# The long filters' matrices re-laid in pairs of steps, and loaded by the rows that have taps

## The reference

```python
v = silu(dwconv(x @ Wv, conv_v))          # q and k likewise
paths = [dwconv(v, fir_s), dwconv(v, fir_m), dwconv(v, fir_l), delta_path, v]
# dwconv: y[t, c] = sum over i of w[c, i] * x[t - (K - 1) + i, c], per channel; K = 3, 15, 64
```

## Time and profile before

| | us |
|---|---|
| median of 3 runs | 971.71 (969.2 to 977.56) |
| the profiled execution | 980.14 |
| its span | 978.3 |
| TensorE busy | 870.4 (89% of the span) |
| TensorE's granted clock over the span | 0.952 of full |
| L666, start of the first to end of the last | 119.0 to 171.7 |

### The profile page before, as it was taken

How to read it: one execution, slowest core, us unless ns; L and a number is a source line. 1 busy time by engine, 2 the same in 40 slices (tenths; PEclk the granted TensorE clock), 3 DMA queues, 4 the chain that set the end, 5 groups by cost and what they waited for, 6 DMA issues and landing times.

```text
span 978.3 us, 18379 instructions
## 1 busy us (share of the span) xinstructions
PE 870.4 (89%) x6875; PEld 654.3 (67%) x6875; DVE 605.2 (62%) x1410; ACT 453.0 (46%) x845; POOL 345.7 (35%) x336
## 2 busy tenths in 40 slices
PE   7799789789999987998889888979997999999994
PEld 5577566667777765786556555656785777777774
DVE  5799797566889888432557777774462343333255
ACT  5788656446677766342144544445331322222221
POOL 9422200123557566312001343223540242222684
PEclk9999999778999997998799999999999999999998
DMA  5699769897455432124991222002302222221421
GB/s 168 202 269 281 203 153 250 296 240 172 109 119 120 76 76 78 32 86 165 388 338 42 63 63 88 12 24 80 100 23 83 66 60 60 66 66 50 151 65 64
DMA packets 144468, 123.52 MB, mean 126 GB/s; under 512 B 89790, under 2 KB 126590, under 8 KB 143102
## 3 DMA queue, kind: packets, MB, share of 16 engines
q1 hardware_dynamic: 140974, 112.98, 41.0%
q0 software_dynamic: 3408, 9.38, 2.6%
HBM read 74.04 MB, written 48.29 MB: 125 GB/s over the span
## 4 chain that ended last, share of the span: by engine, by line
PE 60%; DVE 14%; ACT 10%; POOL 7%; issue 4%; DMA 3%; SPq 1%; POOLq 0%; DVEq 0%; ACTq 0%; another core or an unknown queue 0%
PE ps L2513 10%; PE ps L1919 6%; PE ps L2528 5%; DVE cross_room L1952 4%; PE ps L1859 3%; PE ps L2377 3%; PE ps L1352 3%; PE ps L666 3%; PE ps L1620 3%; POOL hank L345 2%; PE ps L1981 2%; POOL kept L2660 2%; PE ps L2390 2%; PE ps L423 2%; DMA hank<-rt_dram 2%
## 5 line engine op out<-in xcount | busy, mean ns | idle before, releaser
L1997 ACT ACTIVATE cross_room<-ps 128x1024 f32<-128x1024 f32 x64 | 65.5, 1023 | 99.1 <-PE ps L1923 96.9
L1952 DVE TENSOR_REDUCE cross_room<-ps 128x4 f32<-128x1024 f32 x64 | 78.1, 1224 | 39.3 <-PE ps L1919 38.5
L2513 PE MATMUL ps<-wr,xbT 128*128 x312 | 99.0, 459 | 1.8 <-ACT xbT L2549 1.8
L1919 PE MATMUL ps<-kept,cross_room 32*128 32x256 f32 x512 | 74.1, 411 | 21.7 <-DVE cross_room L1952 18.8
L2602 POOL DMA_INDIRECT y_dram<-yb,dest_row x39 | 37.5, 961 | 134.6 <-DVE dest_row L2578 130.4
L1320 POOL TENSOR_TENSOR st<-st,exponent 128x20 f32<-128x20 f32 x16 | 56.9, 3554 | 64.7 <-DVE st L1295 63.4
L2513 PEld LDWEIGHTS ps<-wr,xbT 128*128 128x128 f32 x312 | 58.8, 189 | 29.5 <-issue 2.5
L1923 PE MATMUL ps<-cross_room,kept 32*128 32x256 f32 x512 | 75.3, 413 | 0.0
L1919 PEld LDWEIGHTS ps<-kept,cross_room 32*128 32x128 f32 x512 | 47.1, 190 | 39.7 <-issue 21.7
L550 DVE SCALAR_TENSOR_TENSOR room<-room 128x256 f32<-128x256 f32 x144 | 58.4, 480 | 11.4 <-ACT room L499 11.4
L2587 DVE TENSOR_TENSOR cross_room<-cross_room,ps 128x352 f32<-128x352 f32 x39 | 20.3, 521 | 58.6 <-PE ps L2513 57.1
(11 more groups left out here) (353 smaller groups left out, 2243.2 us busy)
## 6 DMA issues: line engine op xcount, KB each, us to landing
xs_dram<-params SPq DMA_DIRECT2D x17, 1040.0 KB, 17.9
room<-in_gW SPq DMA_DIRECT2D x8, 1280.0 KB, 7.7
tok_dram<-room SPq DMA_DIRECT2D x8, 768.0 KB, 6.4
fir_dram<-room SPq DMA_DIRECT2D x6, 1024.0 KB, 7.3
paths<-fir_dram SPq DMA_DIRECT2D x48, 128.0 KB, 3.7
xb<-xs_dram SPq DMA_DIRECT2D x39, 130.0 KB, 2.3
hank<-rt_dram SPq DMA_DIRECT2D x8, 512.0 KB, 8.1
yr<-y_dram SPq DMA_DIRECT2D x16, 256.0 KB, 3.2
```

The lines of the kernel that those rows point to most:

```text
L1919: m1 = nc.tensor.matmul(ps[:, c, t * T:(t + 1) * T], strips(qS[b % 3], g, c)[:, t * P:(t + 1) * P], kS(b, g)[c * CH:(c + 1) * CH], start=T ...
L1952: V.tensor_reduce(mx[:, :, g, XD + 2 * h * CH:XD + (2 * h + 1) * CH + 1:CH].rearrange("p t c -> p c t"), ps[:, pair(h), :].rearrange("p c ...
L1997: S.activation(pT[g % 2][:, pair(h)].rearrange("p c k t -> p (c k t)"), ps[:, pair(h), :].rearrange("p c n -> p (c n)"), ACT.Exp).then_inc ...
L2513: m = nc.tensor.matmul(ps[:, 2 * (j % 2) + half, 0:FF], xbT[j % 2][:, k, :], wr[:, bass.ds(e, 1), k, half, :].rearrange("p e n -> p (e n)" ...
```

## The change

The 64 steps of a block become 4 blocks of `PER` = 16 steps (index a), each of 8 pairs (index i) of two steps 8 apart (index h): step = 16 a + i + 8 h. `hank` is [128, a, filter, i, channel, h], so that the two steps of a pair are adjacent floats; `rt_dram` rows are twice as wide, holding tap n and tap n + 8 of each channel. The transposes and copies of the filters double to twelve (the second six from `wpad` shifted by 8). The filters lie in `tok[1]` for that time, which gives two new waits in batch 1, and `pe_project` waits for the copies in batch 1 as a third bank is used. A slice is loaded by eight DMAs, four blocks x (64-tap filter; the two short ones), each over the rows in which a filter has taps in that block. The copy out of PSUM and the stores of `stage` follow the new order.

```diff
+LAG = 8
+PER = 2 * LAG
+STEPS_A = BLK // PER
-HANK = ((2, 1, 0, 32), (2, 1, 32, 96), (2, 1, 96, P), (0, 2, 48, 64), (0, 2, 64, 96), (0, 2, 96, P))
+HANK = tuple((f, count, step, P - FIRS[f + count - 1] - PER * step - PER + 1, P - PER * step)
+             for step in range(STEPS_A) for f, count in ((2, 1), (0, 2)))
...
-        filters = views(room3, 0, n_filters, "p (k r f c) -> p k r f c", k=KT, r=RING, f=NF)
-        wpad = views(room3, n_filters, n_filters, "p (k f n) -> p k f n", k=KT, f=NF)
+        filters = tok[1].rearrange("p t j d -> p (t j d)").rearrange("p (k r f c) -> p k r f c", k=KT, r=RING, f=NF)
+        wpad = views(room3, 0, n_wpad, "p (k f n) -> p k f n", k=KT, f=NF)
...
+            pe.wait_ge(s.raw_copied, 3)
+            for n in range(FILTERS):
+                h, k, f = n // (KT * NF), n // NF % KT, n % NF
+                m = nc.tensor.transpose(filter_bank(n), wpad[:, k, f, h * LAG:h * LAG + P], ident[:])
...
+                if j == 2 and b == 1:
+                    pe.wait_ge(s.filters_copied, FILTERS)
...
+            if b == 1:
+                act.wait_ge(s.filters_out, FILTERS_OUT)
             S.copy(tok[i][:, :, 2, :], ps[:, 6, :].rearrange("p (t d) -> p t d", t=TT)).then_inc(*s.v_copied.up())
...
+            if b == 1:
+                dve.wait_ge(s.filters_out, FILTERS_OUT)
...
-                nc.sync.dma_start(env.fir_dram[f, c * NCH:(c + 1) * NCH].rearrange("q (n t) d -> (q n) (t d)", t=BLK),
-                                stage[c][:, f].rearrange("p t d -> p (t d)")).then_inc(*env.fir_out.up(16))
+                nc.sync.dma_start(env.fir_dram[f, c * NCH:(c + 1) * NCH].rearrange("q (n a t) d -> (q n) a (t d)", a=STEPS_A, t=PER),
+                                stage[c][:, :, NF - 1 - f].rearrange("p a t d -> p a (t d)")).then_inc(*env.fir_out.up(16))
...
-                                                 env.hank[sl % RING][:, :, :, q * SL // NCH + pair * 2 + u].rearrange("k f s -> k (f s)"),
+                                                 env.hank[sl % RING][:, :, :, :, q * SL // NCH + pair * 2 + u].rearrange("k a f i h -> k (a f i) h"),
...
-                    S.copy(stage[sl // RING].rearrange("p f t c -> p c f t")[:, c0:c0 + 2, :, ::-1],
-                           ps[:, sl % 2 * PAIRS + pair, 0:2 * NF * BLK].rearrange("p (c f t) -> p c f t", c=2, f=NF)
+                    S.copy(stage[sl // RING].rearrange("p a f (h i) c -> p c (a f) i h", h=2)[:, c0:c0 + 2, ::-1, ::-1, ::-1],
+                           ps[:, sl % 2 * PAIRS + pair, 0:2 * NF * BLK].rearrange("p (c n i h) -> p c n i h", c=2, i=LAG, h=2)
...
-    for f, count, k0, k1 in HANK:
-        s0, s1 = max(0, P - FIRS[f + count - 1] - k1 + 1), min(BLK, P - k0)
-        src = bass.AP(tensor=rt.tensor, offset=((sl * NF + f) * (P + BLK) + s0 + k0) * SL,
-                      ap=[[SL, k1 - k0], [(P + BLK) * SL, count], [1, (s1 - s0) * SL]])
-        nc.sync.dma_start(env.hank[sl % RING][k0:k1, f:f + count, s0:s1, :].rearrange("k f s c -> k f (s c)"),
+    for f, count, step, k0, k1 in HANK:
+        row = 2 * SL
+        src = bass.AP(tensor=rt.tensor, offset=((sl * NF + f) * (P + BLK) + PER * step + k0) * row,
+                      ap=[[row, k1 - k0], [(P + BLK) * row, count], [1, LAG * row]])
+        nc.sync.dma_start(env.hank[sl % RING][k0:k1, step, f:f + count].rearrange("k f i c h -> k f (i c h)"),
                           src).then_inc(*env.hank_in[sl % RING].up(16))
...
-            env.hank = [mem.enter_context(nc.sbuf_tensor(f"hank{i}", [P, NF, BLK, SL], F32)) for i in range(RING)]
+            env.hank = [mem.enter_context(nc.sbuf_tensor(f"hank{i}", [P, STEPS_A, NF, LAG, SL, 2], F32)) for i in range(RING)]
```

More of the change, by code:

```diff
@@ L259, in phase_project_invert_and_fir @@
         n_conv, n_kt, n_sq, n_diag = 3 * KT * T, KT * TT * P, 2 * TT * D, NP * CH
-        n_stage, n_inv, n_filters = NF * BLK * CH, NG * CH * CH, KT * NF * P
+        n_stage, n_inv, n_wpad = NF * BLK * CH, NG * CH * CH, KT * NF * (P + LAG)
         room0 = sb("room0", [P, n_stage])
@@ L269, in phase_project_invert_and_fir @@
         xT = views(room1, n_raw + 2 * n_tok + 2 * n_x, n_x, "p (k t) -> p k t", k=KT)
-        stage = [views(r, 0, n_stage, "p (f t c) -> p f t c", f=NF, t=BLK) for r in (room0, room1)]
+        stage = [views(r, 0, n_stage, "p (a f t c) -> p a f t c", a=STEPS_A, f=NF, t=PER) for r in (room0, room1)]
         room2 = sb("room2", [P, 2 * n_inv])
@@ L283, in phase_project_invert_and_fir @@
         room3 = sb("room3", [P, n_inv])
-        filters = views(room3, 0, n_filters, "p (k r f c) -> p k r f c", k=KT, r=RING, f=NF)
-        wpad = views(room3, n_filters, n_filters, "p (k f n) -> p k f n", k=KT, f=NF)
+        filters = tok[1].rearrange("p t j d -> p (t j d)").rearrange("p (k r f c) -> p k r f c", k=KT, r=RING, f=NF)
+        wpad = views(room3, 0, n_wpad, "p (k f n) -> p k f n", k=KT, f=NF)
         am = views(room3, 0, n_inv, "p (g i j) -> p g i j", g=NG, i=CH)
-        no_taps = env.hank[0][0:BLK, 0, 0:SLICES * NF, :]
+        no_taps = views(env.hank[0][0:BLK].rearrange("k a f i c h -> k (a f i c h)"), 0, SLICES * NF * 2 * SL, "k (n c) -> k n c", n=SLICES * NF)
+        FILTERS, FILTERS_OUT = 2 * KT * NF, 16 * (KT * RING + 1)
         gw1_rows = a["gW1"][D:, :].rearrange("(n g p) c -> p g n c", n=NPATH, p=P)
@@ L313, in sp_weights, with filter_bank @@
                                   a[f"fir{f}"].rearrange("(k p) i -> p k i", p=P)).then_inc(*s.wpad.up(16))
+        def filter_bank(n):
+            return ps[:, (6, 7, 3)[n // 4], n % 4 * P:(n % 4 + 1) * P]
         def pe_filters():
             pe.wait_ge(s.wpad, 16 * NF)
[L319 to L322, removed]
+            pe.wait_ge(s.raw_copied, 3)
+            for n in range(FILTERS):
+                h, k, f = n // (KT * NF), n // NF % KT, n % NF
+                m = nc.tensor.transpose(filter_bank(n), wpad[:, k, f, h * LAG:h * LAG + P], ident[:])
             m.then_inc(*s.filters_turned.up())
@@ L326, in act_filters @@
             act.wait_ge(s.filters_turned, 1)
[L327 to L330, removed]
+            for n in range(FILTERS):
+                h, k, f = n // (KT * NF), n // NF % KT, n % NF
+                S.copy(filters[:, k, :, f, h::2].rearrange("n r (q c) -> n q r c", q=NCH),
+                       filter_bank(n).rearrange("n (q r c) -> n q r c", q=NCH, r=RING)).then_inc(*s.filters_copied.up())
         def sp_filters():
-            sp.wait_ge(s.filters_copied, KT * NF)
+            sp.wait_ge(s.filters_copied, FILTERS)
             for k in range(KT):
@@ L344, in pool_hank_zero @@
                     pool.in_turn()
-                    G.memset(h[:, f].rearrange("k s c -> k (s c)"), 0.0).then_inc(*pool.tick(env.hank_zero))
+                    G.memset(h[:].rearrange("k a f i c h -> k (a f i c h)")[:, f * BLK * SL:(f + 1) * BLK * SL], 0.0).then_inc(*pool.tick(env.hank_zero))
         def sp_first_hank(sl):
@@ L452, in pe_normalise @@
                     pe.wait_ge(s.win_made, b)
-                    pe.wait_ge(s.filters_copied, KT * NF)
+                    pe.wait_ge(s.filters_copied, FILTERS)
                 for t in range(TT):
@@ L771, in sp_hank @@
     nc, rt = pg.nc, env.rt_dram
-    for f, count, k0, k1 in HANK:
-        s0, s1 = max(0, P - FIRS[f + count - 1] - k1 + 1), min(BLK, P - k0)
-        src = bass.AP(tensor=rt.tensor, offset=((sl * NF + f) * (P + BLK) + s0 + k0) * SL,
-                      ap=[[SL, k1 - k0], [(P + BLK) * SL, count], [1, (s1 - s0) * SL]])
-        nc.sync.dma_start(env.hank[sl % RING][k0:k1, f:f + count, s0:s1, :].rearrange("k f s c -> k f (s c)"),
+    for f, count, step, k0, k1 in HANK:
[3 more added lines that the diff above has]
+        nc.sync.dma_start(env.hank[sl % RING][k0:k1, step, f:f + count].rearrange("k f i c h -> k f (i c h)"),
                           src).then_inc(*env.hank_in[sl % RING].up(16))
-        if k1 == P:
+        if f == 0 and step % 2:
             yield
@@ L2700, in decoder_program @@
         env.beta = env.sb("beta", [P, B, NP])
-        env.rt_dram = nc.dram_tensor("rt_dram", [SLICES, NF, P + BLK, SL], F32).ap()
+        env.rt_dram = nc.dram_tensor("rt_dram", [SLICES, NF, P + BLK, 2 * SL], F32).ap()
         env.fir_out, env.hank_zero, env.hank_in = pg.counter(), pg.counter(), [pg.counter() for _ in range(RING)]
```

## The result

| | us |
|---|---|
| after, median of 4 runs | 1144.6 (1140.9 to 1148.39) |
| before on the same chip, median of 4 runs | 973.41 (969.2 to 977.56) |
| ratio | 1.1753 [1.1703, 1.1804] |
| the profiled execution of after, and its span | 1141.66, 1139.9 |

The account below looks back on a forecast made before the run. The prediction took matmuls, filter loads and VectorE's inversion to bound the stretch before the delta phase. Single-engine loads would delay x, tokens and slices, starting that phase 146 us later: 1,126 profiled, 1,118 median, so 1,120 us, range 1,070 to 1,200.

Parts of the forecast that it names:

- Loads on one engine, the same each time: Filter loads: 79 rows is prime, so each such DMA runs on one DMA engine, always the same.
- The share of 1/16: Sign of being right: DMA engines' share near 1/16 for long stretches between 200 and 310 us.
- several 79-row loads were in flight at once: Sign of being wrong: several of the 79-row filter DMAs in flight at the same time.
- The first rival: Filter loads spread or change engines, nothing slow: delta phase could start at 168.3, median 965, 0.7% faster; chance 0.10.
- 81 ns a packet, 27.0 us a slice: Filter loads: one engine at 25.4 GB/s, 81 ns a packet, needs 27.0 us a slice with the short filters.
- the third rival: Filter loads: the lone engine runs at 13.5 GB/s, 51 us a slice, 1,310 us in all; chance 0.04.
- x of batches 5, 6, 7 at 88.5, 121.5, 155: Projection: x waits on the engine behind slices, so its landings come 15, 35 and 55 us late.
- Slice 4 issued at 202: Filter loads: batch 5's token store is 67 us late, moving slice 4's issue from 134.7 to 202.
- Four slices 108 us, filters' end 315, delta phase 316: Last four filter slices take 108 us; filters end at 315, delta phase starts at 316, 146 us later.
- Later phases unchanged: After the delta phase's start: the later phases keep their times.
- Pairs 41 ns a record: Filters' matmuls on TensorE: paired reads cost 41 ns a record instead of 87, busy time 45.1 to about 21 us.
- VectorE is the floor for any gain: Before the delta phase: VectorE inverts until 167.6, so the phase can't start earlier, whatever the filters gain.

Follow-up runs that it names:

- Experiment 1: The changed kernel with its filter loads over 80 and 32 rows instead of 79 and 30; 976.62 us, ratio 1.0047.
- eighth run: The changed kernel with 80- and 32-row loads and two of VectorE's twelve second-inversion rounds moved into the delta phase; 973.79 us, ratio 0.999.
- experiment 7: The changed kernel with 80- and 32-row loads, two inversion rounds moved into the delta phase and only `hank[0]` cleared up front; 972.41 us, ratio 0.996.

## Why the prediction was right

It gave 1,120 us and a range of 1,070 to 1,200; 1144.6 was measured, by the mechanism it named.

- **Loads on one engine, the same each time.** Right: 25 GB/s at 6.6% of sixteen engines, two signals a load; 80 rows remove the loss and prime numbers bring it into the old layout. Two of the prediction's signs need a word. The share of 1/16 holds between the short filters' loads; over 217 to 311 us, with them, it is 0.12. And several 79-row loads were in flight at once, by their issue, which was to be a sign of being wrong; it isn't, since one engine carried them one after another. The first rival, no slow loads, fell with the result. Experiment 1 has loads as that rival had them, and its time of 965 was not reached: 976.6.
- **81 ns a packet, 27.0 us a slice.** 82 ns in the stretch shown. A slice took 28.6: its 332 packets (4 x 79 + 16) are 27.2 by this, 27.6 at the 83 ns of a packet of 2 KB; the rest, some 1 us, has no row. The bound of 51 us, the third rival's, was far off.
- **x of batches 5, 6, 7 at 88.5, 121.5, 155.** The transposes ran at 92.15, 128.87 and 164.58, 4 to 10 us later. The step missed a mechanism: it had x issued at 65.3 and waiting in the engine. It was issued at 82.12, behind eight loads that held SyncE's queue.
- **Slice 4 issued at 202.** At 215.5. The store of tokens and the loads of the last batch went through the held queue one after the other.
- **Four slices 108 us, filters' end 315, delta phase 316.** SyncE was busy with them for 108.55 us, and from the issue to the last copy's end it took 125 us rather than 113: 32.4 until slice 4 had landed, three more at 29, and a last slice of 5.4. The end was 340.3, the start of the delta phase 339.5. Thus 23 us too early, 13.5 of it at the issue of slice 4 and the rest in the four slices.
- **Later phases unchanged.** Right, as far as the medians tell: they lie 171.2 us apart, for a start 169.4 us later. Between the two profiled executions the later phases gave back 8 us (1,126 + 23.5 - 8 = 1,141.5, measured 1,141.66), but that of before was 6.7 us above its median of 973.41 and that of after 2.9 us below its own. So the 25 us from 1,120 to 1144.6 are the late start, and no error of the later phases covered it.
- **Pairs 41 ns a record.** Right (41 in experiment 1), and the copies stayed at 0.84 us (840 ns on the page of after). L682 was busy 33.3 us in after and 28.3 in experiment 1 rather than 21, since records overlap less behind waits, and since they take 80 ns rather than 41 at a granted clock of 0.50, which experiment 1 had from 123.6 to 133.8 us.
- **VectorE is the floor for any gain.** Right: 168.0 and 168.7 in experiment 1, for the 168.3 of the first rival. The eighth run shows that the next floor, the tokens, lies close below. What was wrong in that rival is the step from this start to the time.

## What to carry to other kernels

Before cutting a load down to the rows that matter, factor the number of rows: what counts is its largest divisor up to 16, and a few rows more (80 for 79) are free. In a profile, a large transfer without a time to landing, a DMA share near 1/16 while nothing else runs, and long issues on SyncE are the three marks of it. And before speeding up one engine's part of a stage, find what else ends there: here 82 ns became 41 in parts of a stage, and a VectorE loop that no chain of waits showed, with a load of tokens close behind it, kept the start of the next stage at 168.

## What the runs showed of the hardware

**A queue that is held.** An issue of a `hank` load on SyncE took 0.46 us at the median before and 3.4 at most; behind loads that one engine has to carry every other one took 6.4 to 6.7 us, 7.1 at most. So a lone engine also delays the issue of every transfer behind it in the queue.

**The clock decides the last per cent.** Experiment 1 begins the work behind the filters 4.6 us earlier (168.7 rather than 173.3), and its median shows nothing of it. The two profiled executions do show it: spans of 978.3 and 973.2 at nearly the same mean clock (0.952 and 0.949). Between the medians the clock differs: over the runs of one kernel the time goes with the mean granted clock of the span (correlation -0.92 over the 12 runs of experiment 1, -0.87 over the 23 of before), and the median clock is 0.942 in experiment 1 against 0.957 in before. Runs of before at 0.948 or 0.949 took 977.5 to 986.3 us, those of experiment 1 974.3 to 976.4. Straight lines through the two sets give, as an estimate, 981.9 and 973.3 us at a clock of 0.950. TensorE's work between 142.4 and 160.2 is down from 16.2 us to 11.0, in bursts between waits, and the clock there is 0.90 rather than 1.00:

```profile
142.40:160.20 17.80, 11.01 (x198) 8.64 (x192) 15.99 (x48) 15.84 (x24) 1.90 (x2) 0.90 1.08 202
```

So the saved start was most likely paid for with clock. This is argued from these figures, not shown: no run changed the clock alone.

The same may stand behind the 8 us between the profiled executions of before and after. The windows of the first 60 us of the delta phase (us; busy us of PE, PEld, DVE, ACT, POOL with counts; granted clock; DMA share; GB/s) for before, after and experiment 7:

```profile
170.10:230.10 60.00, 50.07 (x632) 39.39 (x625) 34.18 (x67) 25.85 (x65) 9.70 (x8) 0.74 0.87 242
```

```profile
339.50:399.50 60.00, 46.04 (x638) 37.40 (x637) 35.86 (x68) 28.28 (x66) 9.69 (x8) 0.86 0.90 241
```

```profile
166.50:226.50 60.00, 43.92 (x636) 35.27 (x637) 42.35 (x84) 27.31 (x65) 8.44 (x6) 0.89 0.91 245
```

The granted clock goes from 2.4 GHz to 1.2 and back in this stretch, and stays low for more or less of it. From its start to the first product of the paths' gate (L1406 of before) it took 73.5 us in before, 70.2 in after, 70.2 in experiment 7 and 77.0 in the eighth run, whose clock was 0.71. That is 3 of the 8 us. But the clock doesn't order these times alone: experiment 1 took 73.5 too, at 0.69. After had let TensorE stand still for most of the 100 us ahead of it (18.9 us busy from 240 to 340; clock 0.50 from 263 to 276).

**Open.** Why the clock differs between runs and versions; how many loads the queue takes before it holds the next one; and the 1 us a slice that the packets don't explain.
